# Both entries into the experts: two tiles prepared ahead of the last projection, and the choosing of two groups of tokens moved between slots and tiles

## The reference, cut to what matters

```
gate_scores = einsum('bsd,de->bse', x, gate_w) + gate_b
topk_val, topk_idx = top_k(gate_scores, 2)            # 2 of 24 experts
sparse_gates = softmax(topk_val)
h = gelu(einsum('bsd,edf->besf', x, w1) + b1)         # 128 -> 512
y = einsum('besf,efd->besd', h, w2) + b2              # 512 -> 128
out = sum over the token's two experts of gate * y, + x
```

## Time and profile before

| | |
|---|---|
| median of 3 runs | 1090.13 us |
| profiled execution | 1098.24 us, span 1096.5 us |
| attention A | 0 to 419 us |
| experts, first phase | 419 to 610 us |
| attention B | 610 to 882 us |
| experts, second phase | 895 us to the end |
| mean granted clock of TensorE | 0.955 |

### The profile page before, as it was taken

One profiled execution on the slowest core, in us unless ns is written; L12 is line 12 of the kernel. 1 busy time (PEld: TensorE's weight loads), 2 busy tenths in 40 slices (PEclk: granted clock), 3 DMA queues, 4 the chain that ended last, 5 costly groups with the idle time before them and its releaser, 6 DMA issues.

```text
span 1096.5 us, 28680 instructions
## 1 busy us (share of the span) xinstructions
PE 967.1 (88%) x9400; PEld 756.2 (69%) x9402; DVE 768.2 (70%) x2246; ACT 697.7 (64%) x2121; POOL 734.9 (67%) x1070
## 2 busy tenths in 40 slices
PE   4999999999999897979999989888988749799995
PEld 2555555555556546879999567776766649799995
DVE  3678788888888964635455589899998956344454
ACT  3487877877787764535555567677676645365553
POOL 8664567777676245766666868689999666666564
PEclk8699999999999988989999999899999969899998
DMA  9999984000000005656786299999000056567883
GB/s 338 407 405 406 402 231 150 10 14 14 10 22 12 12 26 165 180 168 189 231 252 186 70 408 406 407 402 301 21 13 21 21 155 185 166 192 215 257 239 102
DMA packets 121872, 203.13 MB, mean 185 GB/s; under 512 B 13300, under 2 KB 67248, under 8 KB 121598
## 3 DMA queue, kind: packets, MB, share of 16 engines
q1 hardware_dynamic: 111470, 184.08, 50.4%
q0 software_dynamic: 9728, 16.95, 4.6%
q10 hardware_dynamic: 528, 0.26, 0.1%
HBM read 76.72 MB, written 127.65 MB: 186 GB/s over the span
## 4 chain that ended last, share of the span: by engine, by line
PE 40%; POOL 19%; DVE 17%; issue 14%; ACT 6%; DMA 1%; POOLq 1%; SPq 1%; DVEq 0%; ACTq 0%
POOL rows_out L1078 12%; PE bank L1740 6%; PE bank L1339 5%; PE bank L1701 5%; PE bank L1661 3%; DVE NMP L1923 3%; POOL SETTLE L1077 3%; POOL rows_in L718 3%; DVE QK L1445 3%; PE bank L1682 3%; PE bank L1656 2%; PE bank L1133 2%; PE bank L1144 2%; PE bank L1719 2%; ACT bank L1400 2%
## 5 line engine op out<-in xcount | busy, mean ns | idle before, releaser
L1110 ACT ACTIVATE QT<-bank,B 128x128 f32<-128x128 f32 x704 | 200.9, 368 | 170.3 <-PE bank L1133 169.4
L1865 ACT ACTIVATE PT<-bank 128x512 f32<-128x512 f32 x320 | 188.3, 603 | 75.2 <-PE bank L1682 74.8
L1078 POOL DMA_INDIRECT rows_out<-Y,XI x176 | 175.2, 995 | 73.3 <-POOL SETTLE L1077 66.1
L1133 PE MATMUL bank<-XIT,PT 128*128 128x128 f32 x1408 | 194.2, 282 | 6.8 <-DVE XIT L1214 6.5
L1144 PE MATMUL bank<-W,QT 128*128 x1408 | 190.5, 279 | 1.3 <-ACT QT L1110 1.3
L1133 PEld LDWEIGHTS bank<-XIT,PT 128*128 128x128 f32 x1408 | 175.2, 196 | 10.6 <-DVE XIT L1214 8.6
L1144 PEld LDWEIGHTS bank<-W,QT 128*128 128x128 f32 x1408 | 175.2, 196 | 1.6 <-issue 1.6
L1275 POOL TENSOR_TENSOR PT<-PT 128x512 f32<-128x512 f32 x128 | 157.9, 1266 | 27.4 <-ACT PT L1384 27.1
L718 POOL DMA_INDIRECT rows_in<-XG,POS x128 | 126.6, 989 | 41.4 <-issue 35.2
L1701 PE MATMUL bank<-KT,QT 48*128 48x384 bf16 (+3 forms) x512 | 123.5, 312 | 13.1 <-DVE NMP L1919 8.3
L1219 DVE TENSOR_TENSOR YB<-bank,B2R 128x128 f32<-128x128 f32 x176 | 51.3, 291 | 110.8 <-PE bank L1144 109.3
(11 more groups left out here) (275 smaller groups left out, 1957.0 us busy)
## 6 DMA issues: line engine op xcount, KB each, us to landing
rows_in<-XI SPq DMA_DIRECT2D x32, 3120.0 KB, 30.9
PT<-in_w_dram SPq DMA_DIRECT2D x176, 256.0 KB
XI<-rows_in SPq DMA_DIRECT2D x176, 65.0 KB
PT<-rows_out SPq DMA_DIRECT2D x31, 256.0 KB, 3.8
W<-in_w2pack_dram SPq DMA_DIRECT2D x4, 1536.0 KB
rows_in<-XI SPq DMA_DIRECT2D x2, 1560.0 KB, 31.3
rows_out<-Y,XI POOLq DMA_INDIRECT x176
X<-in_h_dram SPq DMA_DIRECT2D x8, 256.0 KB, 5.1
```

The source lines that it names most:

```text
L1078: pool.indirect_dma_start(out=rows_out, out_offset=bass.IndirectOffsetOnAxis(ap=XI_I[:, u, D + 1:D + 2], axis=0), in_=Y[:, u % 4, :], in_o ...
L1110: a = act.activation(HT[:, u % 2, c, :], psH[u % 2][:, c * P:(c + 1) * P], ACT.Gelu, bias=B1[:, bass.ds(e * FC + c, 1)])
L1133: mm = pe.matmul(psH[u % 2][:, c * P:(c + 1) * P], W1[:, u, c * P:(c + 1) * P], XIT[:, u % 2, :], start=True, stop=True)
L1865: act.activation(PT[:, m % PT_SLOTS, :], psB[m % 2][:, :], ACT.Exp, scale=float(D) ** -0.5).then_inc(exp_done, 1)
```

## The change

It has five parts.

1. In attention A the first table's 21 DVE steps move from slots 303 to 309 to slots 322 to 328, its PE products from slot 311 to 331 (and from bank 7 to bank 0), and its writing from 313 to 332.
2. At slot 341 PE turns the first two tiles of the experts (`first_turns`) and DVE copies them; both stand ahead of the last projection and its addition to x. PE's up(0) stands right behind that projection. SP loads the rows of tile 0, then (once the last but one unit is done) weights 0 and 1, the rows of tile 1, and weights 2 to 4; before, it loaded four weights ahead of the first rows.
3. In the first tiles group 7's normalization moves from ahead of tile 0 to tile 1 on ACT, and its transposes and logits from tiles 0 and 2 to tiles 3 and 4, in both phases. `head_step` and `route_top` move likewise.
4. At the second table, SP reads it two tiles earlier, at tile 22, and asks for weights 24 to 27 between the rows of 22 and 24 instead of in one run ahead of the rows of tile 24.
5. In attention B group 5's 12 steps of choosing stand in one slot (T = 30), its ranks and places in slot 31, and its 8 sends in slot 32. The first table follows in slots 33 and 34 but for three of its steps. Group 6's ranks and places move into tile 1 of the second phase, and its 8 sends between tiles 1 to 8, one before each scatter.

```diff
+SOON_SLICE = 4 * GROUPS - 1
+FIRST_TURNS, FIRST_COPIES, FIRST_UP = 341, 343, 343
...
-            bank, at = (banks[0], 0) if (ph, late) == (1, 0) else (psG, 0)
+            bank, at = (psG, 0) if late else (banks[0], 0)
...
-            if j == 0:
+            if ph == 1 and j == 1:
+                route_ranks(pe, n - 1)
+            if j == 3:
                 route_transpose(pe, n, 1)
-            if j == 2:
+            if j == 4:
                 route_logits(pe, n)
...
+            if ph == 1 and j == 0:
+                route_power_of_e(pool, n - 1)
+            if ph == 1 and j == 1:
+                route_settle(pool, n - 1)
+            if ph == 1 and 1 <= j < 1 + 2 * GT:
+                route_send(pool, n - 1, 0, (((j - 1) // 2, (j - 1) % 2),))
...
-                if j in (0, EARLY):
-                    for i in range(j, j + WEIGHTS_AHEAD):
-                        ask_for_weights(i)
-                if j + WEIGHTS_AHEAD < EARLY or EARLY <= j < ROW_TILES - WEIGHTS_AHEAD:
+                if j == 1:
+                    ask_for_weights(1)
+                if j == EARLY - 2:
+                    ask_for_weights(EARLY)
+                if 1 < j < EARLY - WEIGHTS_AHEAD or EARLY - 2 <= j < ROW_TILES - WEIGHTS_AHEAD:
                     ask_for_weights(j + WEIGHTS_AHEAD)
...
+        def first_turns(pe, ph):
+            if ph == 0:
+                pe.wait_ge(max_done, STEPS * UNITS)
+            pe.wait_ge(e_tables, 2 * ph + 1)
+            turn(pe, ph, 0, 0)
+            turn(pe, ph, 1, 1)
...
+                if T == SOON_SLICE:
+                    for i in range(4):
+                        route_rows(dve, GROUPS + EARLY_GROUPS - 1, (EARLY_GROUPS - 1) % 2, i)
+                if T == SOON_SLICE + 2:
+                    for i in range(8):
+                        early_step(dve, 1, i)
+                if T == SOON_SLICE + 3:
+                    for i in range(8, 18):
+                        early_step(dve, 1, i)
+                    whole_tables(dve, 1, 0)
...
-                    if g == EARLY_GROUPS - 1 and j == 51:
+                    if g == EARLY_GROUPS - 1 and j == 71:
                         turn_tables(pe, 0, 0)
+                if n == FIRST_TURNS:
+                    first_turns(pe, 0)
+                if n == FIRST_UP:
+                    pe.wait_ge(exp_done, STEPS * UNITS)
+                    up(pe, 0, 0, 0)
...
-                    if g == EARLY_GROUPS - 1 and 43 <= j < 50:
-                        for i in range(3 * (j - 43), 3 * (j - 43) + 3):
+                    if g == EARLY_GROUPS - 1 and 62 <= j < 69:
+                        for i in range(3 * (j - 62), 3 * (j - 62) + 3):
                             early_step(dve, 0, i)
-                    if g == EARLY_GROUPS - 1 and j == 53:
+                    if g == EARLY_GROUPS - 1 and j == 72:
                         whole_tables(dve, 0, 0)
+                if n == FIRST_COPIES:
+                    xi_copy(dve, 0, 0, 0)
+                    xi_copy(dve, 0, 1, 1)
```

More of the change, by code:

```diff
@@ L899, in last_group_act @@
             n = GROUPS * (ph + 1) - 1
-            if j == 0:
+            if ph == 0 and j == 1:
+                for t in range(GT):
+                    route_normalize(act, n, 1, TILES - GT, t)
+            if j == 3:
                 route_copy(act, n)
-            if j == 1:
+            if j == 4:
                 route_second(act, n, 1)
-            if ph == 1 and j == 1:
+            if ph == 1 and j == 5:
                 keep_more(act, n)
-            if ph == 1 and 2 <= j < 2 + GT:
-                keep_scaled(act, n, TILES - GT, (j - 2,))
+            if ph == 1 and 6 <= j < 6 + GT:
+                keep_scaled(act, n, TILES - GT, (j - 6,))
         def last_group_dve(dve, ph, j):
             n = GROUPS * (ph + 1) - 1
-            for i in ((0, 1, 2), (3, 4, 5), (6, 7), (8,), (9,), (10,), (11,), (12,), (13, 14, 15))[j] if j < 9 else ():
+            if ph == 1 and j == 0:
+                for i in (18, 19, 20):
+                    early_step(dve, 1, i)
+            if ph == 1 and j == 1:
+                for i in range(4):
+                    route_rows(dve, n - 1, 0, i)
+            for i in ((), (0, 1), (2, 3, 4), (5, 6, 7), (8,), (9,), (10,), (11,), (12, 13), (14, 15))[j] if j < 10 else ():
                 head_step(dve, ph, i)
-            if 2 <= j < 8:
-                route_top(dve, n, 2 * (j - 2))
-                route_top(dve, n, 2 * (j - 2) + 1)
+            for i in range(12):
+                if j == 4 + i // 3:
+                    route_top(dve, n, i)
             for i in {9: (0,), 10: (1,), 11: (2, 3)}.get(j, ()):
@@ L993, in experts_sp @@
             sp.wait_ge(e_tables, 2 * ph + 1)
-            if ph == 0:
-                sp.wait_ge(pv_done, UNITS - 1)
-            else:
+            if ph == 1:
                 sp.wait_ge(b_prod, 4 * TILES)
@@ L1023, in load @@
                 load_rows(j, u)
+                if j == 0:
+                    if ph == 0:
+                        sp.wait_ge(pv_done, UNITS - 1)
+                    ask_for_weights(0)
+                if j == 1:
+                    for i in range(2, 2 + WEIGHTS_AHEAD):
+                        ask_for_weights(i)
             def ask_for_weights(j):
@@ L1288, in slot @@
                     route_numbers(pool, GROUPS + g - 2, g % 2, GT * (g - 2))
-                if s % GT == 1 and routed(g - 3):
+                if T == SOON_SLICE + 1:
+                    route_settle(pool, GROUPS + EARLY_GROUPS - 1)
+                    route_send(pool, GROUPS + EARLY_GROUPS - 1, 1, [(t, k) for t in range(GT) for k in range(2)])
+                if s % GT == 1 and 0 <= g - 3 < EARLY_GROUPS - 1:
                     route_settle(pool, GROUPS + g - 3)
-                if s % GT > 0 and routed(g - 3):
+                if s % GT > 0 and 0 <= g - 3 < EARLY_GROUPS - 1:
                     rows = (((0, 0), (0, 1), (1, 0)), ((1, 1), (2, 0), (2, 1)), ((3, 0), (3, 1)))[s % GT - 1]
@@ L1343, in slot @@
             def slot(T, s, g):
-                if s % GT == 0 and routed(g - 3):
+                if T == SOON_SLICE:
+                    route_ranks(pe, GROUPS + EARLY_GROUPS - 1)
+                if s % GT == 0 and 0 <= g - 3 < EARLY_GROUPS - 1:
                     route_ranks(pe, GROUPS + g - 3)
@@ L1403, in slot @@
             def slot(T, s, g):
-                if s % GT == 0 and routed(g - 3):
+                if T == SOON_SLICE:
+                    route_exp(act, GROUPS + EARLY_GROUPS - 1)
+                if s % GT == 0 and 0 <= g - 3 < EARLY_GROUPS - 1:
                     route_exp(act, GROUPS + g - 3)
@@ L1481, in slot @@
                 if s % GT == 2 and routed(g - 2):
-                    for i in range(6):
+                    for i in range(12 if g - 2 == EARLY_GROUPS - 1 else 6):
                         route_top(dve, GROUPS + g - 2, i)
```

73 lines of the change are left out of this document (31 added, 42 removed).

## The result

The changed kernel takes 1087.36 us (median of ten; 1082.73 to 1090.63), the kernel before 1093.02 (median of ten; 1087.06 to 1099.60). The ratio is 0.9945, 95% interval 0.9919 to 0.9971: 6.0 us less, between 3.2 and 8.9. A second series gave 0.9937 (0.9911 to 0.9963). The forecast was 1080.6 us, 9.5 us less. The profiled execution of the changed kernel took 1087.17 us, close to its median, with a span of 1085.4. It is set here against the profiled execution of the kernel before, whose span was 1096.5: 11.1 us more, twice what the medians differ by. Where the rest comes from is told with before_again.

What follows compares the result with a forecast made beforehand. Bounds named by place: DVE at attention A's end, POOL's queue in the expert tiles, late rows at tile 24, PE after it. Phase one -9.1 and second entry -0.4 made -9.5, from 1090.13 to 1080.6 us; range 1068 to 1093.

Steps and rivals of the forecast that it cites:

- Part 1: First table moved: -5.4 us in two units of attention A, +2.4 at the first entry, last sum 3.0 earlier.
- its lower bound: End of attention A: -6.4 us if both units lose as much as DVE's steps.
- The wait for the loads behind the table: First entry: rows of tile 1 land late behind the moved table, +1.5 us at the last projection.
- The 2.2 us worked out in the prediction: First entry: landing time of a 65 KB load from fixed cost plus bytes; would make the entry's term about +0.9.
- Parts 2 and 3: Phase one: tiles prepared ahead gain 5.1 us at tile 11; tile 24 turned 7.6 earlier; -9.1 in all.
- the second table's late reading: Tile 24, phase one: second table late at tile 22, a bound of 0 on that part's gain.
- The clock's term: Around tile 24 of phase one: PE's clock fall partly spared, -1.5 us of 0 to -3.4.
- Part 4: Second entry: scatter 0 2.5 us earlier, scatter 15 1.7 later, tile 24's rows as before; -0.4, between -3 and +4.
- Rival B: POOL, both phases: takes the gain back, second phase loses 1; -2 us, 1088 us, chance 0.18.

Runs made afterwards that it cites:

- before_again: The kernel before, unedited, run and profiled a second time; ratio 0.9991 to the kernel before.
- second_half: The kernel before with only the second phase's part of the change, attention B included; 1094.83 us, ratio 1.0015.
- sp24_only: The kernel before with only SP's order at tile 24 changed, in both phases; 1088.76 us, ratio 0.9956.
- first_half: The kernel before with only the first phase's part of the change, attention B and second phase as before; 1083.05 us, ratio 0.9912.
- table_only: The kernel before with only the first table's list, turn and writing moved; 1086.03 us, ratio 0.9935.
- six_ahead: The changed kernel with group 6's ranks, places and eight sends ahead of the second phase's tile 0; 1083.30 us, ratio 0.9909.
- block: The changed kernel with group 6's eight second-phase sends in one block at tile 1; 1089.04 us, ratio 0.9968.
- final: The changed kernel with group 6's sends ahead of tile 0 in phase two, four of them ahead of group 7's deviation in phase one; 1079.09 us, ratio 0.9863.
- after_again: The changed kernel, unedited, run and profiled a second time; ratio 0.9937 to the kernel before.
- rows_first: The kernel `final` with rows of tiles 22 and 23 issued before the second table's reading and the weight requests; 1082.11 us, ratio 0.9889.

## Why the prediction was wrong where it was

**Part 1 was right, and too low.** The units gave 2.1 and 3.9 us, forecast 2.1 and 3.3. The 13.53 at a clock of 0.62 was there in both profiles of before (12.3 in second_half, 13.4 in sp24_only) and 9.7 in each of the twelve with the moved table. For the second unit the sum named the clock alone (only its lower bound had DVE's steps in both). The list had 2.6 us of DVE's work in that unit too, and second_half lets the two be told apart a little: with the list in place but the clock down for only 3.4 us (mean 0.86) the unit still took 12.29. At that rate some 2 of the 3.9 us are the clock's and the rest is the list's; this is an estimate from two windows. The list was to stick out by 1.7 us and cost 0.9; it cost 0.15 that a unit shows (the last is 6.4 us long, before 6.3). The wait for the loads behind the table was to cost 1.5; it cost 0 to 1.8. The rows of tile 1 landed 3.3 us after their issue (408.05 to 411.35), with two weights and a load of rows ahead, below the 3.7 to 4.2 that I took from queues with four weights ahead. The 2.2 us worked out in the prediction from the Trainium skill (DMA: Bandwidth & Descriptors, Anatomy of one DMA) is an estimate for a load alone, from a fit that the Trainium skill gives for DMAs issued by GpSimd; this load is SP's. The row nearest to that case is 1.8 us (470.41 to 472.23), a little less than the estimate.

**Parts 2 and 3: the size right, the reasons half.** Phase one was forecast at -9.1; first_half gave -9.6 (-12.9 to -6.3), and the pair of first profiles -10.2 at the last scatter (613.86 to 603.69). But table_only alone gives 7.1 of it. Scatter 0 of the changed kernel came 4.6 earlier, not 3.0, and scatter 11 6.8 instead of 5.1: the error of part 1 carried along. Y of tile 0 came 11 us earlier, as forecast, but the reasons are these: 6 are the units', some 4 the later place of group 7's steps, and 1 the turned tiles. At tile 24 I had put the second table's late reading down as a bound with a gain of 0. It is what happened in part: a gap of 2.7 us at tile 22 took the place of 4.6 at tile 24. The clock's term was right: 3.4 instead of 6.9 us at 1.2 GHz are worth 1.7, forecast 1.5.

**Part 4 is the step that failed.** "As before ... -0.4" was between first_half and the whole change +3.5 us in the runs, near the +4 end of its bounds. The mechanism stood in the sum, but two terms were mis-sized. Scatter 0 was to come 2.5 us earlier and the stretch to scatter 15 to grow from 36.9 to 41.1; against tile 27's addition the means of the table's first and third row differ by 1.1 and the stretch is 42.1. The missing 1.4 lie in attention B. The window from tile 27's addition to tile 28's, in the changed kernel and then in before_again (columns as above):

```profile
843.69:854.34 10.65, 7.69 (x65) 7.05 (x65) 10.17 (x30) 5.63 (x24) 9.62 (x10) 1.00 0.09 27
```

```profile
849.96:858.37 8.41, 7.53 (x60) 6.81 (x60) 8.14 (x23) 5.70 (x24) 7.63 (x7) 1.00 0.08 26
```

All twelve steps of group 5's choice now stand in it, and DVE is busy for 10.17 of 10.65 us. The last addition comes 2.0 us later in the mean; I had counted 0.7. The 0.9 missing in the stretch are group 6's places: the first send goes 3.65 us behind scatter 0 (891.76 to 895.41), not 2.8. The count behind it was right: 19 operations at 1.32 us make 25.1, and from 895.41 to scatter 11 it took 25.2. At scatter 15 the sum is +4.1 instead of +1.7.

From there to the rows of tile 24 the prediction took back 2.1 us, by letting them go at 948.6 "as before". The profile that it read has 21.5 us from scatter 15 to scatter 24, where the three others with the old order have 19.1 or 19.2. The changed second half takes 16.1 to 17.6, so SP's order gives about 2 against those, and some 2 us of loss are left at scatter 24. The rest of the 3.5 is not pinned down: it lies where executions of one kernel differ as well, and within the interval of the 3.5.

What made the loss is where the eight sends stood. Before the change they ran from 888.07 to 897.89 of before_again's profile, while PE waited for rows and computed tile 0: they were nearly free. Between the tiles they lengthen the stretch from 36.8 to 42.1 us. six_ahead shows it by undoing, block by keeping the late start alone. I had counted what they cost at the new place, and took it for paid by an earlier scatter 0 that came only in part. Rival B had the mechanism ("eight more operations stand between tiles") at +1 for the second phase and 0.18, too little of both. That its 1088 us is near the measured 1087.36 is luck: it had the change at -2, and it was -6.0.

**The base.** The forecast of 1080.6 was 6.8 us too low. Of these 3.5 are the change (-9.5 against -6.0), and most of the rest is the median it was taken from: 1090.13 from three runs, 1093.02 from ten. And the sum was made against one profiled execution, whose second phase was 5 us longer than usual; the rows of tile 24 at 948.67 lie in it. Against that same execution part 4 looks right by luck: from last scatter to last scatter it takes 471.9 us, the changed kernel 471.3. Last, the prediction held a change under 1% for one that a measurement cannot tell from none. Ten runs of each gave an interval of 0.26% either way, enough to see 0.55%.

## What to carry to other kernels

Before work is moved between queues, list the idle time of the queue at the old place and at the new one: an operation costs what it displaces, and eight sends that filled a wait are worth more than the wait they were moved to shorten. Start a serial queue's work as soon as its inputs are there: final, 15.0 us below before, is 8 to 9 below the whole change by this, though 3 to 4 of them only undo what the change had lost. Test the parts of a change one by one: here one move of five gave all of the gain. And take a second profile of the base before a change of half a per cent is reckoned from it.

## What the runs showed of the hardware

- TensorE's clock fell from 2.4 GHz (1.00) to a mean of 0.62, mostly 1.2 GHz, in the unit behind the one in which DVE was busy for 13.4 to 13.5 of 14.0 us, in both profiles of before and in sp24_only, and to a mean of 0.86 in second_half. TensorE had been busy for 11.0 of 14.1 us in the unit ahead of the fall, and for only 0.9 us between 381 and 384 in the first profile. With the list moved that unit takes 12.0 us, TensorE is busy for 10.95 of them, and the clock stayed at 1.00 in the next one in all twelve kernels. The two units together were 6.0 us shorter by 5.4 us less of DVE's work and the kept clock; the clock's share is some 2 us by the estimate above.
- The units of attention A ahead of that place repeat to 0.1 us from run to run. What differs between executions sits in a few places: from the last scatter of phase one to the first addition of attention B 29.7 or 31.4 us in the two profiles of either kernel (28.7 to 31.4 over all), in attention B's slot 8 10.0, 11.6 or 12.4, and between scatters 15 and 21 of the same phase one 11.3 to 13.5 (after_again, six_ahead).
- A load of rows of 65 KB was used 1.8 us after its issue with an idle queue ahead (470.41 to 472.23), 3.2 and 3.3 behind two weights of 256 KB (463.61 to 466.80, 408.05 to 411.35), 3.9 to 4.4 behind four (948.67 to 952.59, 476.97 to 481.20, and 465.92 to 470.31 in rows_first).
- Indirect DMAs on POOL: sends start 1.27 us apart, scatters with their settling step 1.39, a send and a scatter take 2.66.
